# A transformer block on one core: one of two value products moves ahead of the phase's later scores

## The reference

```python
x = x + 0.5 * ffn(layernorm(x))
x = x + attention(layernorm(x))        # 16 heads of 64, the normalisation is applied twice
x = x + 0.5 * ffn(layernorm(x))
# attention:
c_q, c_kv = h @ w_down_q.T, h @ w_down_kv.T
q, k, v = heads(c_q @ w_up_q.T), heads(c_kv @ w_up_k.T), heads(c_kv @ w_up_v.T)
q, k = rope(q), rope(k)
attn = softmax(q @ k.T / 8)
out = (attn @ v) @ w_out.T + residual
```

## Time and profile before

| | |
|---|---|
| time, median of 3 runs | 4093.32 us (4089.73 to 4105.07) |
| the profiled execution: time, span | 4098.04 us, 4096.1 us |
| busy: PE, DVE, ACT, POOL | 95%, 70%, 62%, 72% |
| granted TensorE clock, mean | 0.988 |
| first and last product with values | starts at 576 and 3576 us |

### The profile page before, as it was taken

One profiled execution on the slowest core, in us unless ns is written; L12 is line 12 of the kernel. 1 busy time (PEld: TensorE's weight loads), 2 busy tenths in 40 slices (PEclk: granted clock), 3 DMA queues, 4 the chain that ended last, 5 costly groups with the idle time before them and its releaser, 6 DMA issues. The chain is left out here.

```text
span 4096.1 us, 65749 instructions
## 1 busy us (share of the span) xinstructions
PE 3897.4 (95%) x24908; PEld 2207.7 (54%) x24908; DVE 2849.5 (70%) x3796; ACT 2536.2 (62%) x3191; POOL 2932.8 (72%) x1632
## 2 busy tenths in 40 slices
PE   7999979999999999999999999999999999989999
PEld 6888834444444444444444444444444444478888
DVE  5656567777777776777778777767776777565563
ACT  4455446766766676667666766766676666645544
POOL 3444448878877897888788878878887888634443
PEclk9999989999999999999999999999999999999999
DMA  3233221111211221121122212211211121142331
GB/s 123 99 124 109 81 93 53 60 55 59 83 53 53 71 66 53 61 81 53 53 66 76 63 53 66 68 50 60 86 55 53 58 79 62 33 145 76 125 114 63
DMA packets 192772, 300.36 MB, mean 73 GB/s; under 512 B 50328, under 2 KB 100937, under 8 KB 191817
## 3 DMA queue, kind: packets, MB, share of 16 engines
q1 hardware_dynamic: 192456, 296.17, 22.3%
HBM read 201.20 MB, written 26.73 MB: 56 GB/s over the span
## 5 line engine op out<-in xcount | busy, mean ns | idle before, releaser
L1088 DVE TENSOR_REDUCE atNM<-atPS 128x2 f32<-128x1024 f32 x1024 | 1225.7, 1219 | 452.8 <-PE atPS L899 450.1
L1029 ACT ACTIVATE atPT<-atPS 128x1024 f32<-128x1024 f32 x1024 | 1014.0, 1024 | 773.1 <-PE atPS L920 766.7
L1187 POOL TENSOR_TENSOR atACC<-atACC,atPT 128x1024 f32<-128x1024 f32 x510 | 1238.7, 2429 | 89.3 <-ACT atPT L1029 39.1
L931 PE MATMUL atPO<-atPT,atV 128*64 128x512 f32 x4096 | 1014.2, 602 | 0.0
L1187 POOL TENSOR_TENSOR atACC<-atPT 128x1024 f32<-128x1024 f32 x255 | 606.6, 2379 | 262.8 <-PE atOT L953 181.7
L1020 ACT ACTIVATE atPS<-atSH 128x1024 f32<-128x1024 f32 x683 | 687.4, 1023 | 50.8 <-DVE atNM L1088 34.0
L920 PE MATMUL atPS<-atQH,atKL 64*128 64x512 f32 x2048 | 459.9, 445 | 66.3 <-DVE atPS L1094 51.7
L931 PEld LDWEIGHTS atPO<-atPT,atV 128*64 128x64 f32 x4096 | 259.0, 136 | 456.5 <-issue 433.1
L899 PE MATMUL atPS<-atKH,atQH 64*128 64x512 f32 x2048 | 444.0, 431 | 10.0 <-ACT atQH L1009 7.9
L1094 DVE COPY atPS<-atSH 128x1024 f32<-128x1024 f32 x341 | 418.7, 1228 | 37.9 <-DMA atSH<-atMD 11.4
L920 PE MATMUL atPS<-atQH,atKH 64*128 64x512 f32 x2048 | 406.6, 393 | 0.0
(11 more groups left out here) (278 smaller groups left out, 6461.5 us busy)
## 6 DMA issues: line engine op xcount, KB each, us to landing
atSH<-atMD SPq DMA_DIRECT2D x128, 512.0 KB, 4.3
atVT<-atR SPq DMA_DIRECT2D x508, 128.0 KB, 2.1
f1GB<-f1GD SPq DMA_DIRECT2D x128, 256.0 KB, 6.7
f2GB<-f2GD SPq DMA_DIRECT2D x128, 256.0 KB, 6.8
atRSUM<-atRD SPq DMA_DIRECT2D x126, 256.0 KB, 4.0
X<-x SPq DMA_DIRECT2D x4, 1024.0 KB, 6.0
XS<-x SPq DMA_DIRECT2D x16, 256.0 KB, 3.6
x<-X SPq DMA_DIRECT2D x16, 256.0 KB, 2.3
```

The lines of the kernel that those rows point to most:

```text
L931: ins = pe.eng.matmul(PO[HI[h], :], V[n % 2][:, j, HI[h]], PT[k % NPT][:, h, :], start=j == 0, stop=j == T - 1)
L1029: act.eng.activation(PT[k % NPT][:, :, :], PS[ring.of[step]][:, :, :], ACT.Exp, scale=SCALE).then_inc(grown.sem)
L1088: dve.eng.tensor_reduce(NM[:, q // 4, :, q % 4, t], PS[ring.of[step]][:, :, :], AX.X, ALU.max, negate=True).then_inc(most_out.sem)
L1187: pool.eng.tensor_tensor(total[:, :, :], begun[:, :, :], PT[k % NPT][:, :, :], ALU.add).then_inc(gathered.sem)
```

## The change

In a phase whose first group uses TensorE for none of the six steps in `uses`, while the second group does, and in which tile x is not the first of its half, `attend(x)` and its gather go to the first group, behind `attend(x-1)`. All else keeps its place. The matmuls are the same, in another order.

```diff
--- before.py
+++ after.py
@@ -724,17 +724,25 @@
             def others_of(x):
                 return [step for (tick, _), table in (begin, early, late, end) if tick == x % 2 for step in table.pop(x, [])]
 
+            def uses(steps):
+
+                return [s for s in steps if s[0] in ("turn", "latent", "raise", "value", "sum", "outward")]
+
+
 
             order, held = [], []
             for x in range(-42, 2 * PER * (NN + 4), 3):
                 order += tile("score", x) + most_of(x) + tile("fill", x + 2) + tile("score", x + 1)
-                order += others_of(x) + held + tile("attend", x - 1)
-                order += gathers(held + tile("attend", x - 1))
+                first, one, two = others_of(x), others_of(x + 1), others_of(x + 2)
+                now, later = held + tile("attend", x - 1), tile("attend", x)
+                if x % T and not uses(first) and uses(one + two):
+                    now, later = now + later, []
+                order += first + now + gathers(now)
                 order += most_of(x + 1) + tile("score", x + 2) + most_of(x + 2)
-                now, held = tile("attend", x), tile("attend", x + 1)
+                now, held = later, tile("attend", x + 1)
                 if x % T < T - 1:
                     now, held = now + held, []
-                order += tile("fill", x + 3) + others_of(x + 1) + tile("fill", x + 4) + now + gathers(now) + others_of(x + 2)
+                order += tile("fill", x + 3) + one + tile("fill", x + 4) + now + gathers(now) + two
             assert not any(table for _, table in (begin, early, late, end))
 
             def events(*names):
```

## The result

The changed kernel takes 4118.38 us (median of 6 runs, 4103.10 to 4123.43) against 4094.05 us for the kernel before (6 runs, 4089.73 to 4105.07): ratio 1.0052, with a 95% interval of 1.0038 to 1.0065. That is 24 us slower by the medians and 21 by the ratio, which weighs all the runs. The forecast was 4095 us, in a range of 4080 to 4112. The profiled execution took 4121.15 us, 23.1 more than that of before. Five of the six runs show a mean granted TensorE clock of 0.985 or 0.986 and take 4118 to 4123 us; the sixth shows 0.988, as before, and takes 4103.

What follows compares the result with a forecast made beforehand. TensorE, busy 95%, was taken to bound the kernel through its gaps. Terms 4.2 - 5.7 + 0 + 0 + 0.8 + 2.5 = +1.8 us on the profiled 4098.04 gave 4100; that execution being 4.7 above median, 4095, range 4080 to 4112.

Steps and rivals of the forecast that it cites:

- What S2 does: In changed phases M1 starts 1.87 us and S2 2.21 us after the first product; at x=345 S2 moves 0.17 us back.
- Rest 9, 27, 39, 15: Phases by x mod 48: waits of row, sum and next S0 give +4.2, -5.7, 0 and +0.8 us, in that order.
- The fill's wait: S2's wait on TensorE for VectorE's fill of its bank should fall from 51.7 to below 10 us.
- Rest 3, 0 us: In 22 phases with x mod 48 = 3, S2's gap goes over into the sum's wait for VectorE: 0 us.
- Rest 33, the race: Nine phases, x mod 48 = 33: `qlow` may lose to GpSimd's gather; -2 or +7 us, taken as +2.5.
- the rival of the port: VectorE's delay makes `qlow` lose to gathers in further phases: +38 us, 4131 us, deciding from 17 lost races; chance 0.05.
- The three last phases: At the very end VectorE has less to do; each may save a gap of some 0.6 us, taken as 0 in all.
- The rival of the saved gaps: S2's gaps are simply saved, 0.7 us over 78 phases: -55 us, 4038 us; chance 0.06.

Runs made afterwards that it cites:

- the gather that waits: The full change, with GpSimd's gather of tile x+2 waiting for `qlow` in every third pair: 4106.22 us, ratio 1.0017 against the kernel before.
- the two runs of kinds put together: Kernel before, gather waiting for `qlow`: raise behind sum, product moved at x%48 in (3, 27, 33), 4123.93 us; raise in next phase, (27, 33), 4087.74 us.

## Why the prediction was wrong

- *What S2 does* was right. At x=345 M1 starts 1.86 us after the first product (1.87 forecast), S2 no longer waits, and the second group gives the time back.
- *Rest 9, 27, 39, 15*: each by its own sum. The row at x=345 starts 6.10 us after the first product (6.1 forecast), the S0 behind x=519 5.10 (5.1), and the kinds sum to +5.3, -4.9, -0.05 and +1.2 us (+4.2, -5.7, 0, +0.8). The waits of the row and the sum for the raise grew by 18.0 + 11.4 us and the fill's fell by 30.0, as forecast.
- *The fill's wait*, forecast to fall below 10 us, is 21.7. Of it 9.9 us stand in rest 36, most of them behind lost races (1.9 there with the gather that waits), and 11.1 in rest 0 and 30, which the change leaves as they are (10.8 before).
- *Rest 3, 0 us*, is the step that failed. The gap at S2 did go over into the wait at the sum, and the phase is as long as before: the median differs by 0.01 us. But I gave TensorE's idle time no price where another engine sets the end. The gap at S2 and the wait at the sum became one longer wait, and behind it the clock fell in 9 places and not 3. The runs with the matmuls that add nothing show it: 9 stretches go to none, and the full change gets 14 us faster. Taking rest 3 out of the change gives the same 14 us. By the phases of rest 6, 11.6 us of what the changed kernel takes hang on this, by the times 14; the kernel before pays about 5 of the same kind.
- *Rest 33, the race*: mechanism right, size too small by two thirds. `qlow` lasts 3.44 or 3.45 us in all six phases in which it ran free before, so the gather won every one, at -0.34 and +1.6 to +1.7 us for the two phases, +1.3 each: 8 us, where 2.5 stood in the sum. I took the middle between winning and losing, 2.5, although the starts that I had computed favoured the gather. The rule of the Trainium skill that I cited there (SBUF — State Buffer, Who interferes with whom) gave +7, and the trace agrees: `qlow` lasts 3.44 us with the gather running, 1.21 with the gather behind it.
- *The race outside rest 33*: the rival of the port came true in two phases, x=498 and 882, of the 17 that it needed. Both stand behind a changed phase of rest 15. `qlow` there took 1.22 us before and 3.43 and 3.24 after, and the next phase's sum waits for the raise behind it on VectorE; these are the two phases of rest 21 that got 1.4 and 1.2 us longer. That the move in rest 15 brings them isn't shown: which phases of this kind lose changes from run to run, and the two runs of kinds put together, without that move, have losses there too. VectorE and TensorE after:

```profile
2056.79 3.43 DVE L1091 TENSOR_TENSOR atQL<-atU,atQH 128x1024 fp32r<-128x1024 f32 x1
```

```profile
2061.48 1.07 PE L961 MATMUL atOT<-atACC,atones 128*32 128x512 f32 x8 [1.20 <-DVE atU L1080]
```

- *The three last phases* (x=996, 1002 and 1020) were taken at 0 in all, though each might save its gap of some 0.6 us. At x=996 the gap is saved: with the gather that waits the phase is 0.71 us shorter than before, and the 0.91 us that it is longer in the full change are the lost race of x=993. The other two cost 0.86 each. At x=1002 the first group had two products already, and the second lost one of the two that stood between row and value. The value then waits for ScalarE's copy of the row, which ScalarE does behind a fill. TensorE and ScalarE after, x=1002:

```profile
3545.05 1.09 PE L898 MATMUL atOT<-atWV,atCKV 128*64 128x128 f32 x16 [0.77 <-ACT atML L1022]
```

```profile
3543.80 1.02 ACT L1028 ACTIVATE atPS<-atSH 128x1024 f32<-128x1024 f32 x1
3544.74 0.25 ACT L1022 ACTIVATE atML<-atOT 8x128 f32<-8x128 f32 x1
```

- The rival of the saved gaps did not come, but for x=996: row, sum and S0 do wait.

The sum with rest 33 at its +7 and the last phases at -0.7 + 0.9 + 0.9 would have been about +7 us, inside the range. The clock took the kernel out of it: with the wait filled, or with rest 3 left out, it takes 4104.35 and 4107.40 us, both inside.

## What to carry to other kernels

A gap on the busiest engine is worth filling only if what stands behind it is not waiting too: before a piece of work is moved, write down for each wait behind it what releases it and how late that is. If another engine sets the end, the gap only moves; and if it then joins another gap on TensorE, the longer idle stretch can cost more than either did, through the clock. Where an end is set by two engines whose instructions exclude each other, a shift of hundredths of a microsecond decides over more than one.

## What the hardware showed that I had not expected

In the 22 phases of rest 3, TensorE's idle time ahead of the sum is 1.9 us or more in 6 of the kernel before and in 14 of the one after; half the clock came with it in 3 of the 6 and 9 of the 14, and with no shorter one. The other runs blur this: with rest 3 alone there is one after 1.8 us, with rest 27 alone one after a score's wait of 1.7 us. Where the whole stretch fell into the phase behind, that phase took 9.3 us and not 7.8. What decides between waits that look alike stays open: in the kernel after, the clock fell with one of 1.90 us and not with one of 2.81. That it does not come with each of them would also make the runs of one kernel differ, and the times fit, though only one of these runs has a trace: the changed kernel took 4103 us with a mean clock of 0.988, and 4118 to 4123 with 0.985 or 0.986.
